# Softmax maxima handed to TensorE as two 16-bit parts, with the picks next to each other and the two turns moved

## The chip, the cores and the metric

The kernel runs on one core of a Trainium2 chip. The metric is the device time of the whole program in microseconds (us), the median of several runs. All times below are microseconds unless they are marked ns. Engines are named as the profile names them: PE (TensorE matmuls), PEld (its weight loads), DVE (VectorE), ACT (ScalarE), POOL (GpSimd), SP (SyncE).

## What is computed

A cross-attention over 32 batches, and then a feed-forward block over the tokens that a router picks. Only the attention is touched by the change. Per batch there are 112 queries and 375 context rows, 257 of an image and 118 of a text, with two separate softmaxes whose results are added:

```python
q = rms_norm(linear(x, q_w, q_b), norm_q_w).reshape(B, L, NH, HD)
k = rms_norm(linear(ctx_txt, k_w, k_b), norm_k_w).reshape(B, -1, NH, HD)
v = linear(ctx_txt, v_w, v_b).reshape(B, -1, NH, HD)
k_img = rms_norm(linear(ctx_img, k_img_w, k_img_b), norm_k_img_w).reshape(B, -1, NH, HD)
v_img = linear(ctx_img, v_img_w, v_img_b).reshape(B, -1, NH, HD)
img_x = attention(q, k_img, v_img)
txt_x = attention(q, k, v)
out = (txt_x + img_x).reshape(B, L, DIM)
return linear(out, o_w, o_b)
```

There are 16 heads of 32 numbers each, the model width is 512, everything is float32. The kernel needs the softmax's maximum of every query, head and kind of context, and subtracts it before the exponential.

## The kernel before

The 16 heads are worked on in NG = 4 groups `g` of GH = 4 heads. Phase 1 is a loop over 32 batches. Each engine has its own program, whose order is written out by hand (`body` for batches 0 to 30, of which 2 to 29 are a hardware loop, and `last` for batch 31). The programs meet only through counting semaphores: `wait_ge(semaphore, number)`. In `body(i, n, m, p, q)`, `i` is the batch in work, `n` the next one (its context is projected to keys in the same stretch), `p` and `q` the two before it (their outputs are finished there).

What a batch needs, and which engine does it:

- `scores(i, g)` (PE, L1625): queries times keys of four heads into PSUM banks 2 to 5, queries on the partitions. It serves for the maxima only.
- `group_max(i, g)` (DVE, L1151 and L1152): two reductions that read these banks, text and image maxima, into the tile `top[e]`, e = g // 2. Each head has 32 columns in `top`, of which two for each group are used. The next `scores` waits for it, since it uses the same banks.
- `turn_top(i, e)` (PE, L1636, and a copy on ACT, L834): transposes `top[e]` into `topT[e]`, so that the maxima of a head lie on its own 32 partitions. On PE there is one such turn in front of `scores(i, 3)` and one in front of `scores_T(i, 0)`.
- `scores_T(i, g)` (PE): the scores again, now with keys on the partitions. Into each PSUM bank go first the maxima with a minus sign: `topT` as the moving operand against a constant matrix that holds -1 in the rows of the wanted maximum, `pick_c` (L1660, 119 columns, text and the last image row) and `pick_img` (L1664, 128 columns). The products of keys and queries (L1654) are added on top. The matrices are held for all of the four groups and loaded anew for each matmul.
- `exps(i, g)` (ACT, L843 and L845), `sum_image` (POOL, L581, adds the two image parts of the probabilities), `add_tail` (DVE, L1157, adds the last image row), `weighted_values` (PE, L1691, in which the part with `prob_img` gives the image's sum), `normalise` (DVE, L1163, L1165, L1169), `o_hi` (ACT, L863) and `o_rest` (DVE, L1173) that make the high and the low part of the attention's result.
- `keys`, `values` and `output` (PE, L1535 to L1537): projections in three matmuls, high by high, low by high and high by low, which need `ctx_hi` (ACT, L780) and `ctx_lo` (POOL, `split_ctx`, L547, in two parts: `ctx_lo(0)` with 472 elements a partition and `ctx_lo(1)` with 1024). `keys(n, 1)` to `keys(n, 3)` need the second part. `add_bias` (DVE, L1131), `squares` (ACT, L813), `inverse_rms` (POOL, L574) and `scale_k` (DVE, L1137) finish the keys.
- `score(q)` and `ranks(q)` (DVE, L1200, L1191, L1193), `turn_score` (PE, L1641) and, in batch 30 alone, a count (PE, L1733) belong to the router. `output` and `residual` on POOL (L585, L589) are additions of 112 x 512.

PE's order in a batch is scores 0, weighted values 2 and 3 of the batch before, scores 1, values, scores 2, values, turn 0, scores 3, keys 0, turn 1, `scores_T` 0, keys 1, the score's turn, `scores_T` 1, keys 2, `scores_T` 2, weighted values 0 and 1, `scores_T` 3, output, turns, values. The waits that matter here are

```python
def scores_T(i, g):
    if g == 0:
        pe.wait_ge(s_done, 4 * i + 4)
    else:
        pe.wait_ge(exp_done, 8 * i + 2 * g)
    if g % 2 == 0:
        pe.wait_ge(topT_ready, 2 * i + 1 + g // 2)
```

## Time and profile before

| | before |
|---|---|
| median of 3 runs | 1529.23 (1525.77 to 1529.79) |
| the profiled execution | 1524.64 |
| its span, first to last instruction | 1522.9 |
| mean granted clock of PE | 0.999 |
| PE busy | 1497.2, 98% |
| PEld busy | 1186.7, 78% |
| DVE busy | 1182.6, 78% |
| ACT busy | 715.8, 47% |
| POOL busy | 688.5, 45% |

The span is that of one profiled execution, which took 1.7 more around it. The busy share is the time in which an instruction of that engine ran, also where the instruction itself was held up. The clock is the share of PE's full speed that it was granted.

### The profile page before, as it was taken

The page shows a single profiled execution, that of the slowest core. Times are in us where ns is not written, and L with a number is a line of the kernel's source. Part 1 is how long each engine was busy: PE and PEld are TensorE (multiplying, and loading weights), DVE is VectorE, ACT ScalarE, POOL GpSimd, SP SyncE. Part 2 cuts the span into 40 slices and gives each one's busy share as a digit, 9 for nine tenths or more (in the row PEclk, how much of TensorE's full clock was granted, in tenths as well). Part 3 has the DMA queues.
Part 4 walks back from the last instruction along what each step waited for, and adds up shares of the span by engine and source line. Part 5 has one row for each costly group of instructions (what it writes and reads, how often), then busy time and mean ns, then how long its engine had stood idle before and what let it go on. Part 6 is the DMA issues. An engine that isn't in the chain of part 4 may idle for free.

```text
span 1522.9 us, 41381 instructions
## 1 busy us (share of the span) xinstructions
PE 1497.2 (98%) x16220; PEld 1186.7 (78%) x16220; DVE 1182.6 (78%) x1884; ACT 715.8 (47%) x1458; POOL 688.5 (45%) x727
## 2 busy tenths in 40 slices
PE   8999999999999999999999999999999999999997
PEld 6777777777777777777777777777777787778997
DVE  6765788888888888888888888888887686554986
ACT  5874444444444444444444444444445124655431
POOL 3543344454444454444444444544445692114752
PEclk9999999999999999999999999999999999999999
DMA  8961121211111221112221112121125524010000
GB/s 262 346 207 60 39 63 52 77 56 50 56 54 59 67 66 50 56 50 62 62 70 50 56 50 62 58 75 50 56 87 154 196 111 167 28 56 29 1 1 25
DMA packets 70199, 121.04 MB, mean 79 GB/s; under 512 B 21840, under 2 KB 36528, under 8 KB 68608
## 3 DMA queue, kind: packets, MB, share of 16 engines
q1 hardware_dynamic: 69312, 117.54, 23.9%
q0 software_dynamic: 832, 2.75, 0.7%
q8 instruction: 36, 0.59, 0.2%
q14 instruction: 19, 0.16, 0.0%
HBM read 89.93 MB, written 30.34 MB: 79 GB/s over the span
## 4 chain that ended last, share of the span: by engine, by line
PE 89%; DVE 5%; ACT 3%; issue 1%; DMA 1%; POOL 1%; ACTq 0%; DVEq 0%; POOLq 0%
PE ps L1535 21%; PE ps L1536 19%; PE ps L1537 18%; PE ps L1691 10%; PE ps L1654 6%; PE ps L1625 3%; PE ps L1596 3%; PE ps L1660 2%; PE ps L1900 2%; PE ps L1917 2%; PE ps L1909 1%; PE ps L1664 1%; DMA q_dram<-q_turned 1%; DVE rec L1163 1%; PE ps L1636 0%
## 5 line engine op out<-in xcount | busy, mean ns | idle before, releaser
L547 POOL TENSOR_TENSOR ctx_lo<-ctx_raw,ctx_hi 128x472 fp32r<-128x472 f32 (+1 forms) x62 | 112.8, 1819 | 192.8 <-ACT ctx_hi L780 192.8
L1163 DVE RECIPROCAL rec<-ps 128x224 f32<-128x224 f32 x128 | 198.3, 1549 | 1.1 <-PE ps L1691 0.9
L581 POOL TENSOR_TENSOR prob_img<-prob 128x448 f32<-128x448 f32 x93 | 107.9, 1160 | 149.3 <-ACT prob L845 149.3
L1152 DVE TENSOR_REDUCE top<-ps 112x4 f32<-112x1028 f32 x128 | 156.2, 1220 | 0.0
L1151 DVE TENSOR_REDUCE top<-ps 112x4 f32<-112x472 f32 x128 | 83.1, 649 | 72.9 <-PE ps L1625 72.9
L1654 PE MATMUL ps<-q_all,k_all 32*128 32x112 f32 (+1 forms) x3072 | 125.2, 274 | 0.0
L1535 PE MATMUL ps<-w_v_img_hi,ctx_hi 128*128 128x512 f32 x256 | 107.4, 419 | 0.0
L1535 PE MATMUL ps<-w_k_img_hi,ctx_hi 128*128 128x512 f32 x256 | 107.1, 418 | 0.0
L843 ACT ACTIVATE prob<-ps 119x448 f32<-119x448 f32 x96 | 52.4, 546 | 114.8 <-PE ps L1654 114.8
L1654 PEld LDWEIGHTS ps<-q_all,k_all 32*128 32x128 f32 (+1 forms) x3072 | 105.4, 184 | 0.0
L1536 PE MATMUL ps<-w_k_img_lo,ctx_hi 128*128 128x512 f32 x256 | 101.1, 395 | 0.0
L1536 PE MATMUL ps<-w_v_img_lo,ctx_hi 128*128 128x512 f32 x256 | 101.0, 395 | 0.0
L1537 PE MATMUL ps<-w_k_img_hi,ctx_lo 128*128 128x512 f32 x256 | 100.8, 394 | 0.0
L1537 PE MATMUL ps<-w_v_img_hi,ctx_lo 128*128 128x512 f32 x256 | 100.7, 393 | 0.0
L845 ACT ACTIVATE prob<-ps 128x896 f32<-128x896 f32 x96 | 87.7, 913 | 0.0
L780 ACT ACTIVATE ctx_hi<-ctx_raw 128x472 fp32r<-128x472 f32 x64 | 52.9, 827 | 69.8 <-PE ps L1537 69.8
L1137 DVE SCALAR_TENSOR_TENSOR proj<-proj,rstd,w_img 128x512 f32<-128x512 f32 x64 | 48.0, 750 | 45.4 <-POOL rstd L574 45.4
L1537 PE MATMUL ps<-hT_hi,ring_lo 128*128 128x448 f32 x224 | 81.9, 366 | 0.0
L813 ACT ACTIVATE sq_junk<-proj 128x513 bf16<-128x513 f32 (+1 forms) x96 | 61.1, 636 | 34.8 <-DVE proj L1131 34.8
L574 POOL TENSOR_TENSOR rstd<-sq_sum,neg_half 128x1 f32<-128x1 f32 x96 | 64.8, 675 | 16.0 <-ACT sq_junk L813 16.0
L1173 DVE SCALAR_TENSOR_TENSOR oT_lo<-o_space,oT_hi 128x448 fp32r<-128x448 f32 x31 | 39.7, 1282 | 40.7 <-ACT oT_hi L863 40.7
L1157 DVE SCALAR_TENSOR_TENSOR prob_img<-prob,ones_last,prob_img 23x448 f32<-23x448 f32 x93 | 64.5, 693 | 6.1 <-POOL prob_img L581 3.1
(358 smaller groups left out, 4410.7 us busy)
## 6 DMA issues: line engine op xcount, KB each, us to landing
ctx_raw<-in_ctx_dram SPq DMA_DIRECT2D x32, 748.0 KB, 4.2
xh_dram<-xh SPq DMA_DIRECT2D x32, 448.0 KB
xc<-in_xT_dram SPq DMA_DIRECT2D x28, 256.0 KB, 4.5
q_dram<-q_turned SPq DMA_DIRECT2D x28, 256.0 KB, 4.6
q_all<-q_dram SPq DMA_DIRECT2D x32, 224.0 KB, 3.1
out_dram<-out_sb SPq DMA_DIRECT2D x32, 224.0 KB, 2.3
xh<-in_x_dram SPq DMA_DIRECT2D x31, 224.0 KB, 2.9
proj<-in_x_dram SPq DMA_DIRECT2D x21, 256.0 KB, 5.1
```

The source lines that it names most:

```text
L547: nc.gpsimd.tensor_tensor(ctx_lo[:, :, cols], ctx_raw[:, :, cols], ctx_hi[:, :, cols].bitcast(F32), ALU.subtract).then_inc(ctx_lo_done, 1)
L574: nc.gpsimd.tensor_tensor(rstd1[:, k:k + 1], sq_sum[:, k:k + 1], neg_half[:], ALU.pow).then_inc(rms_inv, 1)
L581: nc.gpsimd.tensor_tensor(prob_img[:, g % 2], image[:, 0, :], image[:, 1, :], ALU.add).then_inc(img_summed, 1)
L845: nc.scalar.activation(image.rearrange("p c (j q) -> p j c q", j=GH), ps[:, 2:6, L:3 * L].rearrange("p j (c q) -> p j c q", c=2), ACT.Exp) ...
L1151: nc.vector.tensor_reduce(rows[:, :, 2 * g], ps[0:L, 2:6, 0:TXT], AX.X, ALU.max)
L1152: nc.vector.tensor_reduce(rows[:, :, 2 * g + 1], ps[0:L, 2:6, TAIL:CTX], AX.X, ALU.max).then_inc(s_done, 1)
L1163: nc.vector.reciprocal(rec[:], bank[:, 2:4]).then_inc(norm_step, 1)
L1535: nc.tensor.matmul(o_, a_hi, b_hi, start=start, stop=False)
L1536: nc.tensor.matmul(o_, a_hi, b_lo, start=False, stop=False)
L1537: return nc.tensor.matmul(o_, a_lo, b_hi, start=False, stop=stop)
L1654: made = nc.tensor.matmul(ps[0:rows, 2 + j, c * L:(c + 1) * L], k_all[head, g, at:at + rows], q_all[head, g, :], start=False, stop=stop)
L1691: last = nc.tensor.matmul(ps[HD * j:HD * (j + 1), bank, slot * L:(slot + 1) * L], left[0:rows, cols], right[0:rows, L * j:L * (j + 1)], st ...
```

## The change

The maxima go to PE in two 16-bit parts. After every second group DVE rounds the 16 new maxima of each query to bfloat16 (`top_hi`) and writes maximum minus rounded maximum into 16 columns of `top` that were unused; `topT`, `pick_c` and `pick_img` become bfloat16, and each column of a pick matrix has two rows of -1, so that high and low part are added again in the PSUM bank. The `pick_img` matmuls stand directly behind the `pick_c` ones. On PE the first turn stays in front of `scores(i, 3)` and waits for the split; the second moves behind `keys(n, 1)`, in front of the score's turn; ACT's copy of it moves behind `squares(n, 1)`. In `last` some steps of POOL, PE, ACT and DVE change places. Two unused tiles (`pick_gap`, `top_gap`) keep the addresses of all other tiles as they were.

```diff
...
         ctx_hi = p1("ctx_hi", [P, KC, CTXC], F32R)
         ctx_lo = p1("ctx_lo", [P, KC, CTXC], F32R)
         proj = p1("proj", [P, 3, D + 1])
-        pick_c = p1("pick_c", [P, NG, CHUNK_C], F32R)
-        pick_img = p1("pick_img", [P, NG, P], F32R)
+        pick_c = p1("pick_c", [P, NG, CHUNK_C], BF16)
+        pick_img = p1("pick_img", [P, NG, P], BF16)
+        p1("pick_gap", [P, NG * (CHUNK_C + P) // 2])
         under_qT = ExitStack()
         cos_tab, sin_tab = (under_qT.enter_context(nc.sbuf_tensor(n, [L, P], F32)) for n in ("cos_tab", "sin_tab"))
         normed_last = under_qT.enter_context(nc.sbuf_tensor("normed_last", [L, D], F32))
...
         ones_last = p1("ones_last", [CHUNK_C, HD])
         ones_all = p1("ones_all", [P, HD])
         top = [p1(f"top{e}", [L, P]) for e in range(2)]
-        topT = [p1(f"topT{e}", [P, L], F32R) for e in range(2)]
+        topT = [p1(f"topT{e}", [P, L], BF16) for e in range(2)]
+        top_hi = p1("top_hi", [L, GH * 4], BF16)
+        p1("top_gap", [P, L - 8])
         prob_img = p1("prob_img", [P, 2, GH * L])
         nq_row = prob_img[:].rearrange("p a n -> p (a n)")[:, 0:D]
         prob = p1("prob", [P, 2, 3, GH * L])
...
                 for c in range(EARLY):
                     gather(c)
                 output(q)
+                residual(p)
                 pool.wait_ge(oT_lo_done, i)
+                pool.wait_ge(top_split, 2 * i + 2)
                 value_weights_lo(0, 0)
+                normalise_h(p)
                 value_weights_lo(0, 1).then_inc(w_lo_done, 1)
-                residual(p)
-                normalise_h(p)
                 token_roots(slice(0, EARLY), 1)
                 output(p)
                 pool.wait_ge(xres_loaded, 16 * i + 16)
...
                 split_ctx(n, 1)
                 value_image(i, 1)
                 turn_top(i, 0)
-                turn_top(i, 1)
                 exps(i, 0)
                 if p is not None:
                     o_hi(p)
                 squares(n, 1)
+                turn_top(i, 1)
                 exps(i, 1)
                 squares(n, 2)
                 exps(i, 2)
...
                 token_squares(0)
                 value_image(i, 1)
                 token_squares(1)
+                exps(i, 0)
                 turn_top(i, 1)
-                exps(i, 0)
                 token_squares(2)
                 exps(i, 1)
                 exps(i, 2)
...
                 rows = top[g // 2][:].rearrange("l (j r) -> l j r", j=GH)
                 nc.vector.tensor_reduce(rows[:, :, 2 * g], ps[0:L, 2:6, 0:TXT], AX.X, ALU.max)
                 nc.vector.tensor_reduce(rows[:, :, 2 * g + 1], ps[0:L, 2:6, TAIL:CTX], AX.X, ALU.max).then_inc(s_done, 1)
+
+            def split_top(i, e):
+                rows = top[e][:].rearrange("l (j r) -> l j r", j=GH)
+                high, low = rows[:, :, 4 * e:4 * e + 4], rows[:, :, 2 * NG + 4 * e:2 * NG + 4 * e + 4]
+                dve.wait_ge(s_done, 4 * i + 2 * e + 2)
+                nc.vector.tensor_copy(top_hi[:].rearrange("l (j r) -> l j r", j=GH), high).then_inc(top_rounded, 1)
+                dve.wait_ge(top_rounded, 2 * i + e + 1)
+                nc.vector.scalar_tensor_tensor(low, high, 1.0, top_hi[:].rearrange("l (j r) -> l j r", j=GH), ALU.mult, ALU.subtract).then_inc(top_split, 1)
 
             def add_tail(i, g):
                 dve.wait_ge(img_summed, 4 * i + g + 1)
...
                 else:
                     dve.wait_ge(pro_full, 2)
                     nc.vector.tensor_copy(v_tail, ps[0:B, 6, :]).then_inc(pro_done, 1)
+                split_top(i, 0)
                 group_max(i, 2)
                 if q is not None:
                     score(q)
                 group_max(i, 3)
+                split_top(i, 1)
                 if p is not None:
                     normalise(p, 3)
                 add_bias(n, 1)
...
                 group_max(i, 0)
                 o_rest(p)
                 group_max(i, 1)
+                split_top(i, 0)
                 score(q)
                 group_max(i, 2)
                 group_max(i, 3)
+                split_top(i, 1)
                 add_residual(p)
                 ln2(p)
                 ranks(q)
...
                 last.then_inc(s_full, 1)
 
             def turn_top(i, e):
-                pe.wait_ge(s_done, 4 * i + 2 * e + 2)
+                pe.wait_ge(top_split, 2 * i + e + 1)
                 if e:
                     pe.wait_ge(topT_ready, 2 * i + 1)
                 if not isinstance(i, int) or i:
...
                 for j in range(GH):
                     head = slice(HD * j, HD * (j + 1))
                     nc.tensor.matmul(ps[0:CHUNK_C, 2 + j, 0:L], pick_c[head, g, :], topT[g // 2][head, :], start=True, stop=False)
-                products(0, True)
                 for j in range(GH):
                     head = slice(HD * j, HD * (j + 1))
                     nc.tensor.matmul(ps[:, 2 + j, L:3 * L].rearrange("p (c q) -> p c q", c=2), pick_img[head, g, :],
-                                     topT[g // 2][head, :].unsqueeze(1).to_broadcast([HD, 2, L]), start=True, stop=False)
+                                     topT[g // 2][head, :].unsqueeze(1).to_broadcast([HD, 2, L]), start=False, stop=False)
+                products(0, False)
                 products(1, False)
                 products(2, True).then_inc(st_full, 1)
 
...
                 turn_top(i, 0)
                 scores(i, 3)
                 keys(n, 0)
-                turn_top(i, 1)
                 scores_T(i, 0)
                 keys(n, 1)
+                turn_top(i, 1)
                 if q is not None:
                     pe.wait_ge(pv_done, 4 * i)
                     turn_score(q)
...
                 values(i, 2, range(3, 4))
                 values(i, 1, range(0, 2))
                 scores(i, 2)
-                turn_top(i, 0)
                 values(i, 1, range(2, 3))
                 output(p, range(0, 2))
+                turn_top(i, 0)
                 scores(i, 3)
                 values(i, 1, range(3, 4))
                 output(p, range(2, 4))
-                turn_top(i, 1)
                 scores_T(i, 0)
                 pe.wait_ge(pv_done, 4 * i)
                 turn_score(q)
                 pe.wait_ge(b0_done, value_slot(i, 1)[3] + 1)
                 fill(0, 10)
+                turn_top(i, 1)
                 scores_T(i, 1)
+                pe.wait_ge(topT_ready, 2 * i + 2)
                 weighted_values(i, 0, None)
                 scores_T(i, 2)
                 pe.wait_ge(rank_done, q + 1)
...
     for w in ("wq", "wk", "wv", "wo", "w_gate", "w_up", "w_down"):
         arrays[w] = c(a[f_ + w])
     token = np.arange(L)
-    arrays["pick_rows"] = -(np.arange(P)[:, None] % HD == np.arange(2 * NG)[None, :]).astype(f)
+    parts = (np.arange(2 * NG)[None, :], 2 * NG + np.arange(2 * NG)[None, :])
+    arrays["pick_rows"] = -sum((np.arange(P)[:, None] % HD == part).astype(f) for part in parts)
     arrays["slot_far"] = np.broadcast_to(np.arange(TOPK, dtype=f) - f(FAR), (L, TOPK)).copy()
     arrays["token_no"] = token.astype(f)[:, None].copy()
     arrays["token_base"] = (L * (BPC * np.arange(NC)[None, :] + token[:, None] // TOPK)).astype(f)
```

On DVE, in the loop's body, before: from the end of `normalise(p, 2)` to the third instruction of `normalise(p, 3)`.

```order
L1169 SCALAR_TENSOR_TENSOR o_space<-o_two,v_bias 128x112
L1147 REGISTER_ALU
L1151 TENSOR_REDUCE top<-ps 112x4
L1152 TENSOR_REDUCE top<-ps 112x4
L1199 ISA
L1200 SCALAR_TENSOR_TENSOR out_sb,score_now<-xh,wr 112x512
L1147 REGISTER_ALU
L1151 TENSOR_REDUCE top<-ps 112x4
L1152 TENSOR_REDUCE top<-ps 112x4
L1161 REGISTER_ALU
L1163 RECIPROCAL rec<-ps 128x224
```

The same stretch of the changed kernel, whose line numbers are higher by 5 to 13; L1163 is the rounding here, L1165 the low part, and L1156 and L1157 are the reductions.

```order
L1182 SCALAR_TENSOR_TENSOR o_space<-o_two,v_bias 128x112
L1163 CAST top_hi<-top 112x16
L1164 REGISTER_ALU
L1165 SCALAR_TENSOR_TENSOR top<-top,top_hi 112x4x4
L1152 REGISTER_ALU
L1156 TENSOR_REDUCE top<-ps 112x4
L1157 TENSOR_REDUCE top<-ps 112x4
L1212 ISA
L1213 SCALAR_TENSOR_TENSOR out_sb,score_now<-xh,wr 112x512
L1152 REGISTER_ALU
L1156 TENSOR_REDUCE top<-ps 112x4
L1157 TENSOR_REDUCE top<-ps 112x4
```

One split now stands between `normalise(p, 2)` and the reductions of group 2; the other comes right behind the last of these rows, in front of `normalise(p, 3)`.

On PE, before: the end of `keys(n, 0)`, the second turn and `scores_T(i, 0)`.

```order
L1537 MATMUL ps<-w_k_hi,ctx_lo 118x512
L1636 MATMUL ps<-ident,top 128x112
L1660 MATMUL ps<-topT,pick_c 119x112 x4
L1654 MATMUL ps<-q_all,k_all 119x112 x4
L1664 MATMUL ps<-topT,pick_img 128x224 x4
L1654 MATMUL ps<-q_all,k_all 128x112 x8
```

The changed kernel, from the same place:

```order
L1554 MATMUL ps<-w_k_hi,ctx_lo 118x512
L1677 MATMUL ps<-topT,pick_c 119x112 x4
L1680 MATMUL ps<-topT,pick_img 128x224 x4
L1671 MATMUL ps<-q_all,k_all 119x112 x4
L1671 MATMUL ps<-q_all,k_all 128x112 x8
L1552 MATMUL ps<-w_k_img_hi,ctx_hi 128x512
```

The turn is gone from here, and the two picks (L1677, L1680) are neighbours. Behind `keys(n, 1)`, in batch 30, the changed kernel has

```order
L1554 MATMUL ps<-w_k_img_hi,ctx_lo 128x512
L1653 MATMUL ps<-ident,top 128x112
L1658 MATMUL ps<-ident,score_now 112x112
L1750 MATMUL ps<-chosen,later 112x24
L1677 MATMUL ps<-topT,pick_c 119x112 x4
```

where L1653 is the second turn and was not there before; the score's turn (L1658) and the count (L1750) stood alone.

## Rows read from the trace of the kernel before

**Rows 1.** The page's part on the chain that ended last.

```profile
PE 89%; DVE 5%; ACT 3%; issue 1%; DMA 1%; POOL 1%; ACTq 0%; DVEq 0%; POOLq 0%
```

**Rows 2.** Busy time by stretches, one whole batch; columns as in its head line.

```profile
core 0: us, PE busy (x) PEld busy (x) DVE busy (x) ACT busy (x) POOL busy (x), PEclk, DMA share, GB/s
...
714.30:747.08 32.78, 32.78 (x436) 25.66 (x435) 27.05 (x41) 15.03 (x29) 14.97 (x16) 1.00 0.19 58
```

**Rows 3.** Timeline of PE, one batch: start us, duration us, instruction.

```profile
723.68 0.26 PE L1636 MATMUL ps<-ident,top 112*128 112x112 f32 x1
...
723.87 0.43 PE L1625 MATMUL ps<-k_hi,q_hi 32*112 32x376 f32 x4
...
727.12 0.26 PE L1636 MATMUL ps<-ident,top 112*128 112x112 f32 x1
...
727.31 0.32 PE L1660 MATMUL ps<-topT,pick_c 32*119 32x112 f32 x4
...
728.36 0.50 PE L1535 MATMUL ps<-w_k_img_hi,ctx_hi 128*128 128x512 f32 x1
...
738.68 0.38 PE L1691 MATMUL ps<-prob_img,ones_all 128*32 128x112 f32 x8
```

**Rows 4.** Timeline of DVE, the same batch.

```profile
721.56 0.64 DVE L1151 TENSOR_REDUCE top<-ps 112x4 f32<-112x472 f32 x1
...
722.12 1.22 DVE L1152 TENSOR_REDUCE top<-ps 112x4 f32<-112x1028 f32 x1
...
728.07 0.34 DVE L1169 SCALAR_TENSOR_TENSOR o_space<-o_two,v_bias 128x112 f32<-128x112 f32 x1
...
730.36 1.31 DVE L1173 SCALAR_TENSOR_TENSOR oT_lo<-o_space,oT_hi 128x448 fp32r<-128x448 f32 x1 [1.35 <-ACT oT_hi L863]
...
736.12 0.75 DVE L1137 SCALAR_TENSOR_TENSOR proj<-proj,rstd,w_img 128x512 f32<-128x512 f32 x1 [1.43 <-POOL rstd L574]
...
736.90 0.68 DVE L1157 SCALAR_TENSOR_TENSOR prob_img<-prob,ones_last,prob_img 23x448 f32<-23x448 f32 x1
```

**Rows 5.** Timelines of DVE and PE in the last batch, where PE waits.

```profile
1146.01 1.22 DVE L1152 TENSOR_REDUCE top<-ps 112x4 f32<-112x1028 f32 x1
...
1147.28 0.43 PE L1625 MATMUL ps<-k_hi,q_hi 32*112 32x376 f32 x4 [0.35 <-DVE top L1152]
```

**Rows 6.** Timeline of POOL, the batch of rows 3.

```profile
721.71 1.22 POOL L547 TENSOR_TENSOR ctx_lo<-ctx_raw,ctx_hi 128x472 fp32r<-128x472 f32 x1 [5.73 <-ACT ctx_hi L780]
...
725.27 2.42 POOL L547 TENSOR_TENSOR ctx_lo<-ctx_raw,ctx_hi 128x1024 fp32r<-128x1024 f32 x1
...
730.03 1.16 POOL L581 TENSOR_TENSOR prob_img<-prob 128x448 f32<-128x448 f32 x1 [2.34 <-ACT prob L845]
...
738.20 1.15 POOL L581 TENSOR_TENSOR prob_img<-third_img 128x448 f32<-128x448 f32 x1 [2.11 <-ACT third_img L845]
```

**Rows 7.** Weight loads: groups by form, one line's range, and a timeline.

```profile
L1664 PEld LDWEIGHTS ps<-topT,pick_img 32*128 32x128 f32 x512 | 25.2, 187 | 0.0
...
L1660 PEld LDWEIGHTS ps<-topT,pick_c 32*119 32x119 f32 x512 | 23.5, 173 | 34.4 <-issue 33.8 <-ACT prob L845 0.6
...
L1901 PEld LDWEIGHTS ps<-causal,ident_bf x64: 128/130/132, 1249.4 to 1380.4; 112*112 112x112 bf16 x64
...
702.70 0.18 PEld L1660 LDWEIGHTS ps<-topT,pick_c 32*119 32x119 f32 x4 [0.36 <-issue]
...
703.00 0.20 PEld L1664 LDWEIGHTS ps<-topT,pick_img 32*128 32x128 f32 x4
```

**Rows 8.** Timeline of PE in batch 30.

```profile
1124.71 0.17 PE L1733 MATMUL ps<-chosen,later 112*112 112x24 bf16 x1
...
1124.82 0.32 PE L1660 MATMUL ps<-topT,pick_c 32*119 32x112 f32 x4
```

**Rows 9.** The instructions of line 1143.

```profile
L1143 DVE CAST k_hi<-k_tail x32: 171/172/174, 122.3 to 1138.2; 128x4 fp32r x28, 128x4 fp32r<-128x4 f32 x4
```

**Rows 10.** One line's range, then timelines of DVE and POOL.

```profile
L1173 DVE SCALAR_TENSOR_TENSOR oT_lo<-o_space,oT_hi x31: 615/1310/1311, 173.2 to 1147.1; 128x448 fp32r<-128x448 f32 x31
...
1147.14 0.61 DVE L1173 SCALAR_TENSOR_TENSOR oT_lo<-o_space,oT_hi 128x448 fp32r<-128x448 f32 x1
...
1181.98 1.00 DVE L1272 TENSOR_SCALAR chosen<-rank 112x8 bf16<-112x8 f32 x1
...
1181.67 1.28 POOL L710 TENSOR_TENSOR ring_lo<-ring,ring_lo 128x512 fp32r<-128x512 f32 x1
```

## The prediction on record

> **What bounds the kernel now.** I read the chain of waits first: TensorE (PE) holds 89% of the chain that ended last [rows 1]. Then two neighbouring batches in the table by stretches: a batch takes 32.78 us and PE is busy for 32.78 of them at a granted clock of 1.00, while VectorE (DVE) has 27.05 and GpSimd (POOL) 14.97 [rows 2]. So in the loop (batches 2 to 29) nothing is gained except by PE doing less, and anything that makes PE wait is paid in full, 28 to 30 times over. Third, the timelines, to see how late each maximum comes. The reader is to see in [rows 3, 4] that the second reduction for group 2 ends at 722.12 + 1.22 = 723.34 and that `scores(i, 3)`, which waits for it (its PSUM banks), starts at 723.87: 0.53 later. From end to start such a hand-over needs 0.05 where PE really waited (1146.01 + 1.22 = 1147.23, PE starts at 1147.28) [rows 5]. **The slack in front of the last score group is 0.48 us.** In the same way `keys(n, 1)` at 728.36 needs POOL's `ctx_lo`, which ends at 725.27 + 2.42 = 727.69 [rows 3, 6]: slack 0.67, less the hand-over.
>
> **Weight loads (gain).** Per `scores_T` the four loads of pick_c and the four of pick_img become 16-bit; there are 32 x 4 = 128 calls. Loads now: 173 ns (119 columns) and 187 ns (128 columns), while a 16-bit load of 112 columns took 130 [rows 7]. Passes follow each other every 0.10 us there (three from 702.70 to 703.00), though 112 columns stream in far less, so the loads set the pace [rows 7]. Scaled to 112 columns the 32-bit load is about 174, so 16 bits save some 44 ns at 112 columns, 0.39 ns a column; 119 + 128 columns give 0.097 us, **0.10 us a `scores_T`**, 0.41 a batch with rounding, 12.8 in all. Bounds: 0, if what counts is only the number of columns, and 0.15 (18.7 in all), if these loads vanish behind the streams. I take 0.10, from the nearest row. The Trainium skill ("TensorE: Matmul & The Clock Gate", section on LDWEIGHTS, loading the stationary operand) gives a load's time by its columns alone, columns / 1.2 in ns; by that rule this term is 0. The trace has 187 and 130 ns for a difference of 16 columns, which speaks against it. The reordering of the picks adds and removes no matmul: 0.
>
> **The moved turn.** The second turn costs 727.31 − 727.12 = 0.19 where it stands, of which a change of shape that `scores_T` has anyway is, as an estimate, 0.09: 0.10. Beside the score's turn it costs again about 0.10, as the count matmul between the same two neighbours does (1124.71 to 1124.82) [rows 3, 8]. Net 0, bounds −0.05 and +0.05. Once, in batch 30, that count matmul waits for `topT_ready`, which now comes after the second turn: +0.4.
>
> **The split on DVE.** Four instructions a batch. Alone each is as short as a cast of 128x4, 0.17 us [rows 9], and follows its neighbour with 0.04 or so for the semaphore: together 0.29 to 0.38. That would fit into the slack of 0.48. The question is whether they run alone. [Rows 10] are the evidence that they don't. L1173, a DVE instruction with two SBUF inputs, took 1.31 in the loop, with POOL's L581 running beside it (730.03 + 1.16 = 731.19 [rows 6]), and 0.61 in the last batch: it ended 0.48 after POOL's end. A DVE conversion of 112x8 to 16 bits, which should take about 0.17, took 1.00 and ended when POOL's L710 (1181.67 + 1.28) did. So one engine's instruction stands still until the other's is over. DVE's reductions, fed from PSUM, kept 0.65 and 1.22 next to L547. The new cast and subtraction are of the kind that stands still, and `split_top(i, 0)` comes at 721.56, exactly where POOL's L547 starts, at 721.71 [rows 4, 6]. 
>
> Step by step, on the clock of the batch at 714.30:
> - Cast 721.56 to 721.73. The subtraction can ask at 721.77; POOL has begun at 721.71 and holds until 722.93. It ends at 722.96. Group 2's reductions begin at 722.88 instead of 721.56, +1.32. Less the slack: **`scores(i, 3)` +0.84**.
> - The score and POOL's output addition follow, so `ctx_lo(1)` starts at 726.59 and not 725.27, and ends at 729.00. `keys(n, 1)` is due at 728.36 + 0.84 − 0.10 (load) − 0.11 (turn moved) = 728.99 and starts at 729.09: **+0.10**.
> - `split_top(i, 1)` finds that same `ctx_lo(1)` running and is held until 729.0. `normalise(p, 3)` starts at 729.15, and its third instruction (728.07 before [rows 4]) ends at 731.95 instead of 728.41, held for a while by L581. DVE is now 3.5 late; most of its idle time of 1.35 ahead of L1173 and the 0.70 that L1173 no longer loses take 1.9 of that back. But `scale_k(n, 1)` now meets POOL's residual addition and loses 0.5, so everything behind runs +2.15: `scale_k(n, 2)` 736.12 → 738.27, `add_tail(i, 1)` 736.90 → 739.05.
> - POOL's L581 for group 2 follows PE, not DVE: 738.20 → 739.01. It gets in first by 0.04 us and holds `add_tail(i, 1)`, which ends at 740.16 − 0.13 + 0.68 = 740.71. PE's image part of group 1 is due at 738.68 + 0.84 + 0.10 − 0.30 (three `scores_T`) = 739.32 and waits until 740.78: **+1.46**.
> - DVE enters the next batch late, `scores(i + 1, 1)` waits a little: **+0.08** (0 to 0.1).
>
> Per batch: 0.84 + 0.10 + 1.46 + 0.08 − 0.41 = **+2.07**. Batches 2 to 30 are 29: 60.0. Batch 0 has no `ctx_lo` in the way (−0.4), batch 1 part of it (+0.5), batch 31 has no next context (−0.3), and +0.4 of the count: +0.2. Profiled run: 1524.64 + 60.2 = 1584.8. The profiled run lies 4.6 below the median of the three runs, 1529.23, so the forecast for the median is **1589**. ACT's work and SP's queues are not changed; ACT's second topT copy moves behind squares(n, 1), into idle time, and costs nothing unless exps(i, 1) came 0.26 later (PE takes it 3 us later).
>
> **Rivals.**
> - A: as above, but `add_tail(i, 1)` wins the last race (it lost by 0.04). It then ends at 739.73 and PE waits 0.44 and not 1.46: about +1.05 a batch, 1529.2 + 30 = **1560**. For it: the tiny margin; against: each of the ends is given to 0.01 and batches repeat to that.
> - B: the subtraction wins against L547 (it lost by 0.06; if a 16-bit cast is shorter or POOL needs longer to start). Then only split 1 is held, DVE is late by less, and `add_tail(i, 1)` still meets L581: about +1.2, **1564**.
> - C, the other side: no hold at all for operations this small, since 16 elements a partition may be through before POOL takes its first. Split 0 costs 0.29 to 0.38, under the 0.48 of slack; `ctx_lo(1)` comes 0.38 later, under 0.67; only the loads remain: 1529.2 − 12.4 = **1517**. It turns on the single question of whether split 0 ends before 723.34 + 0.48 − 1.78 = 722.04. Against it: the 1.00 for 112x8.
> - D: loads of 16 bits are no faster (the rule by columns), with the holds as forecast: 1589 + 12.8 = **1602**.
> - E: one race won and the loads as forecast, or C without faster loads: gains and losses cancel, **1529**.
>
> **How the numbers follow.** Forecast 0.48 (own range 1581 to 1597), A 0.17, B 0.12, D 0.07, C 0.11, E 0.05. Two runs of this kernel can be told apart from about 0.3%, 4.6 us. Faster: C, 0.11. Same: E, 0.05. Slower: the rest, 0.84. The range leaves out C and E: from under A to just above D, 1553 to 1605.
>
> **What the profile after would show.** The split's subtraction at about 1.2 us in the loop and below 0.2 in batch 0; a mean of the cast far over 0.2, since every second one meets `ctx_lo(1)`. PE idle 0.8 to 0.9 before the last score group with DVE's reduction as releaser, and about 1.4 before the image part of group 1. Pick loads at 130 to 140 ns and `scores_T` in 0.95 us. A period of 34.85. Rival C shows itself by casts and subtractions at 0.17 and a period near 32.35; A by an idle time of 0.4 in place of 1.4; D by unchanged loads. The prediction is wrong above all if small operations slip past POOL.

## The result

The changed kernel takes 1647.93 us (median of 4; 1645.76 to 1650.04), the kernel before 1527.89 beside it: ratio 1.0785, 95% interval 1.0769 to 1.08. It is slower, as forecast, but by 120.0 us where the prediction had 60: the time lies outside the range of 1553 to 1605.

| | before | after |
|---|---|---|
| median | 1527.89 | 1647.93 |
| span of the profiled execution | 1522.9 | 1647.3 |
| mean granted clock of PE | 0.999 | 0.974 |
| PE's share of the chain [rows 1] | 89% | 55% |

The page of the changed kernel, first the busy times, then the shares of the chain that ended last:

```profile
PE 1530.3 (93%) x16220; PEld 1196.6 (73%) x16220; DVE 1351.0 (82%) x2012; ACT 713.8 (43%) x1458; POOL 689.8 (42%) x727
...
PE 55%; DVE 17%; issue 15%; POOL 6%; ACT 4%; DMA 2%; DVEq 0%; POOLq 0%; ACTq 0%
```

DVE is busy 168 us more, for 128 small instructions that were meant to take 0.17 each, 22 in all. That is the first hint that instructions stand still inside. PE's waits say where the time is lost:

```profile
PE ps L1708 <- DVE prob_img L1170: 60.6, 29, 2.2
PE ps L1642 <- DVE top L1157: 23.4, 31, 0.8
```

These are the two waits of the forecast, before the image part of group 1 (L1708) and before a score group (L1642), as total, number and longest. The second is near what was foretold (0.77 a batch for 0.8 to 0.9), the first is 2.15 in the median of the loop and not 1.46. One batch, DVE, then POOL, then PE (start us, duration us). It begins at 746.74, so 32.44 is to be taken off to compare with the clock of [rows 3, 4, 6] and of the forecast:

```profile
754.02 0.17 DVE L1163 CAST top_hi<-top 112x16 bf16<-112x16 f32 x1
754.22 1.22 DVE L1165 SCALAR_TENSOR_TENSOR top<-top,top_hi 112x16 f32<-112x16 f32 x1
755.36 0.64 DVE L1156 TENSOR_REDUCE top<-ps 112x4 f32<-112x472 f32 x1
...
759.49 2.02 DVE L1163 CAST top_hi<-top 112x16 bf16<-112x16 f32 x1
761.54 0.17 DVE L1165 SCALAR_TENSOR_TENSOR top<-top,top_hi 112x16 f32<-112x16 f32 x1
...
767.18 2.56 DVE L1142 SCALAR_TENSOR_TENSOR proj<-proj,rstd,w_txt 118x512 f32<-118x512 f32 x1
...
772.54 1.55 DVE L1170 SCALAR_TENSOR_TENSOR prob_img<-prob,ones_last,prob_img 23x448 f32<-23x448 f32 x1
```

```profile
754.18 1.22 POOL L551 TENSOR_TENSOR ctx_lo<-ctx_raw,ctx_hi 128x472 fp32r<-128x472 f32 x1 [4.63 <-ACT ctx_hi L785]
...
759.07 2.40 POOL L551 TENSOR_TENSOR ctx_lo<-ctx_raw,ctx_hi 128x1024 fp32r<-128x1024 f32 x1
...
766.79 1.29 POOL L593 TENSOR_TENSOR xh<-xh,out_bias 112x512 f32<-112x512 f32 x1
768.04 1.14 POOL L585 TENSOR_TENSOR prob_img<-prob 128x448 f32<-128x448 f32 x1
...
772.49 1.12 POOL L585 TENSOR_TENSOR prob_img<-third_img 128x448 f32<-128x448 f32 x1 [0.77 <-ACT third_img L850]
```

```profile
757.19 0.43 PE L1642 MATMUL ps<-k_hi,q_hi 32*112 32x376 f32 x4 [0.77 <-DVE top L1157]
...
760.71 0.82 PE L1671 MATMUL ps<-q_all,k_all 32*119 32x112 f32 x24
...
771.60 0.38 PE L1708 MATMUL ps<-prob,ones_txt 119*32 119x112 f32 x8
774.15 0.40 PE L1708 MATMUL ps<-prob_img,ones_all 128*32 128x112 f32 x8 [2.18 <-DVE prob_img L1170]
...
774.74 1.47 PE L1671 MATMUL ps<-q_all,k_all 32*119 32x112 f32 x24
...
776.14 0.77 PE L1552 MATMUL ps<-w_o_hi,oT_hi 128*112 128x512 f32 x1
```

Each long DVE row ends with a POOL row: the subtraction at 755.44 (POOL 755.40), the cast at 761.51 (761.47), the tail addition at 774.09, 0.48 after POOL's 773.61, like L1173 in [rows 10]. `scale_k(n, 1)` (767.18) ends at 769.74, 0.56 after the end not of the first but of the second POOL instruction beside it. The last PE rows show something else: the 24 product matmuls of a group take 0.82 at 760.71 and 1.47 here, and the first 512-column matmul of a projection 0.77 and not 0.50 [rows 3]. The granted clock in this batch, and in the microseconds after the wait (after the duration of the stretch come the busy times of PE, PEld, DVE, ACT and POOL, then the clock, here 0.95, 0.80, 0.50, 0.50, 1.00, then the DMA share and GB/s):

```profile
746.74:784.04 37.30, 34.28 (x437) 26.40 (x436) 33.64 (x47) 15.03 (x29) 15.70 (x18) 0.95 0.17 51
774.00:775.00 1.00, 0.85 (x24) 0.68 (x28) 0.97 (x3) 0.07 (x1) 0.00 (x0) 0.80 0.00 0
775.00:776.00 1.00, 1.00 (x24) 0.94 (x20) 1.00 (x1) 0.66 (x2) 0.27 (x1) 0.50 0.00 0
...
777.00:778.00 1.00, 1.00 (x4) 0.63 (x4) 1.00 (x3) 0.63 (x1) 0.21 (x1) 0.50 0.20 17
778.00:779.00 1.00, 1.00 (x6) 0.77 (x5) 1.00 (x1) 0.00 (x0) 0.94 (x1) 1.00 0.83 207
```

PE stood still from 771.97 to 774.15, and after it was granted its lower level of 1.2 GHz for some 3.4 us. Measured from one scores 0 to the next, the 28 batches of the loop take either some 35.67 us (6 batches, without such a stretch) or some 37.23 (22 batches, with one). The fall does not follow every wait of this length: the stretch from 205.06 to 240.76 has a wait of 2.14 and a clock of 1.00. The kernel before has such a standstill too, once, outside of the loop, and at a clock of 1.00:

```profile
157.13 0.43 PE L1625 MATMUL ps<-k_hi,q_hi 32*112 32x376 f32 x4 [2.13 <-ACT k_all L822]
```

All kernels of this document stand still at this place, for 2.1 to 2.4 us; the clock falls there in seven of the traces (the changed kernel's among them) and not in the other six. What decides it stays open.

### The profile page after: what moved, and what is told of

Its sections match the earlier page's. It is cut to its first block, busy times and chain, and to the rows that moved or that the text cites. A ratio compares the mean times of both kernels' runs of the same rounds, so it can differ in the third digit from the quotient of the medians.

```text
span 1647.3 us, 41594 instructions
## 1 busy us (share of the span) xinstructions
PE 1530.3 (93%) x16220; PEld 1196.6 (73%) x16220; DVE 1351.0 (82%) x2012; ACT 713.8 (43%) x1458; POOL 689.8 (42%) x727
## 4 chain that ended last, share of the span: by engine, by line
PE 55%; DVE 17%; issue 15%; POOL 6%; ACT 4%; DMA 2%; DVEq 0%; POOLq 0%; ACTq 0%
PE ps L1552 12%; PE ps L1553 11%; PE ps L1554 11%; PE ps L1708 6%; DVE top L1157 4%; POOL prob_img L585 4%; DVE rec L1176 4%; PE ps L1671 3%; DVE prob_img L1170 3%; PE ps L1613 2%; PE ps L1642 2%; PE ps L1918 2%; PE ps L1935 2%; ACT prob L850 2%; DVE top L1156 1%
## 5 line engine op out<-in xcount | busy, mean ns | idle before, releaser
L1157 DVE TENSOR_REDUCE top<-ps 112x4 f32<-112x1028 f32 x128 | 156.0, 1219 | 0.0
L585 POOL TENSOR_TENSOR prob_img<-prob 128x448 f32<-128x448 f32 x93 | 116.3, 1250 | 90.3 <-ACT prob L850 90.3
L1156 DVE TENSOR_REDUCE top<-ps 112x4 f32<-112x472 f32 x128 | 82.9, 648 | 63.7 <-PE ps L1642 63.5
L1671 PE MATMUL ps<-q_all,k_all 32*128 32x112 f32 (+1 forms) x3072 | 111.2, 278 | 0.0
L1708 PE MATMUL ps<-prob_img,ones_all 128*32 128x112 f32 x992 | 47.7, 263 | 60.6 <-DVE prob_img L1170 60.6
L1671 PEld LDWEIGHTS ps<-q_all,k_all 32*128 32x128 f32 (+1 forms) x3072 | 99.5, 192 | 0.0
L1170 DVE SCALAR_TENSOR_TENSOR prob_img<-prob,ones_last,prob_img 23x448 f32<-23x448 f32 x93 | 88.8, 955 | 5.6 <-POOL prob_img L585 2.6
```

What stands on the lines that cost most here:

```text
L585: nc.gpsimd.tensor_tensor(prob_img[:, g % 2], image[:, 0, :], image[:, 1, :], ALU.add).then_inc(img_summed, 1)
L1156: nc.vector.tensor_reduce(rows[:, :, 2 * g], ps[0:L, 2:6, 0:TXT], AX.X, ALU.max)
L1157: nc.vector.tensor_reduce(rows[:, :, 2 * g + 1], ps[0:L, 2:6, TAIL:CTX], AX.X, ALU.max).then_inc(s_done, 1)
L1170: nc.vector.scalar_tensor_tensor(prob_img[last_rows, g % 2], prob_of(g)[0][last_rows], ones_last[last_rows, 0:1], prob_img[last_rows, g % ...
L1671: made = nc.tensor.matmul(ps[0:rows, 2 + j, c * L:(c + 1) * L], k_all[head, g, at:at + rows], q_all[head, g, :], start=False, stop=stop)
L1708: last = nc.tensor.matmul(ps[HD * j:HD * (j + 1), bank, slot * L:(slot + 1) * L], left[0:rows, cols], right[0:rows, L * j:L * (j + 1)], st ...
```

## Experiments

Eleven kernels. The first four were to separate cause and place.

**split_alone**: the splits added to the kernel before, nothing else.

```diff
                 nc.vector.tensor_copy(v_tail, ps[0:B, 6, :]).then_inc(pro_done, 1)
+                split_top(i, 0)
                 group_max(i, 2)
...
                 group_max(i, 3)
+                split_top(i, 1)
```

> The kernel before with the two splits put into VectorE's order where the change has them, writing to tiles that nothing reads; TensorE, ScalarE and GpSimd are those of before. Theory (the splits are held by GpSimd's ctx_lo, VectorE comes late for the rest of the batch, and TensorE's clock falls after the long wait): the loss is all here and the loads' gain is missing, 1650 to 1670 us, with waits of about 0.8 us before the last score group and about 2 us before the image part of group 1. Rival (the loss is TensorE's: 16-bit picks among 32-bit matmuls, or the moved turn): 1528 us. Rival (VectorE merely has 0.3 to 0.4 us more to do twice a batch): 1528 to 1545 us.

Measured: 1664.85 us, ratio 1.0914 (1.0896 to 1.0932), period 37.57, waits of 0.77 and 2.03, clock 0.970. The clock falls in 27 of the 28 batches of the loop, after waits shorter than the 2.12 to 2.19 of the changed kernel: the length of the wait alone does not decide. The whole loss and more comes from two short DVE pairs whose output nobody reads. TensorE's part of the change is not to blame.

**no_split**: the opposite; the low part is left out, so the maxima that are subtracted are rounded ones. In `body`, and in the same way in `last`:

```diff
-                split_top(i, 0)
                 group_max(i, 2)
...
-                split_top(i, 1)
...
-                pe.wait_ge(top_split, 2 * i + e + 1)
+                pe.wait_ge(s_done, 4 * i + 2 * e + 2)
```

> The changed kernel without the splits: the maxima go to TensorE rounded to 16 bits, the low part is left out (it stays zero), all else is as changed. Theory: the gain of the loads alone, 0.41 us a batch, 1515 us (1509 to 1519). Rival (the loss is TensorE's own): about 1640. Rival (16-bit loads bring nothing): 1528.

Measured: 1514.04 us, ratio 0.9919 (0.9902 to 0.9935), period 32.33 for 32.78. The gain term holds: 12 to 13 us. The changed kernel's loads are 125 and 131 ns, for 173 and 187 in [rows 7] (duration min/median/max after the colon):

```profile
L1677 PEld LDWEIGHTS ps<-topT,pick_c x512: 124/125/171, 140.8 to 1284.9; 32*119 32x119 bf16 x171
...
L1680 PEld LDWEIGHTS ps<-topT,pick_img x512: 130/131/187, 140.8 to 1284.9; 32*128 32x128 bf16 x171
```

**psum_split**: same places in the order, other forms of instruction (the waits between them and the form of the last batch are left out here).

```diff
-                nc.vector.tensor_copy(top_hi[...], high).then_inc(top_rounded, 1)
-                nc.vector.scalar_tensor_tensor(low, high, 1.0, top_hi[...], ALU.mult, ALU.subtract).then_inc(top_split, 1)
+                nc.vector.tensor_reduce(rounded, high.unsqueeze(3), AX.X, ALU.max).then_inc(top_rounded, 1)
...
+                in_bank = ps[0:L, 7, 448:464].rearrange("l (j r) -> l j r", j=GH)
+                nc.vector.tensor_reduce(in_bank, rounded.unsqueeze(3), AX.X, ALU.max).then_inc(top_rounded, 1)
...
+                nc.vector.scalar_tensor_tensor(low, high, 1.0, in_bank, ALU.mult, ALU.subtract).then_inc(top_split, 1)
```

> The changed kernel, the splits at the same places but in a form that has never two operands in SBUF and no cast: a reduction over one element rounds, a second one puts the rounded part into PSUM, and the subtraction reads it there; three instructions for two, 0.17 each. (The last batch keeps the SBUF operand.) Theory (held at the port that VectorE shares with GpSimd): no instruction of the split takes over 0.25 us; 0.55 to 0.6 us stand in a slack of 0.48, so 1515 to 1530 us. Rival (VectorE's added work by itself, or its place in the order): 1640 or more.

Measured: 1521.24 us, ratio 0.997 (0.996 to 0.9981), period 32.57. Its DVE groups (busy, then mean ns of one):

```profile
L1168 DVE TENSOR_REDUCE ps<-top_hi 112x16 f32<-112x16 bf16 x62 | 11.1, 178 | 2.1
L1164 DVE TENSOR_REDUCE top_hi<-top 112x16 bf16<-112x16 f32 x64 | 10.6, 166 | 1.1
L1173 DVE SCALAR_TENSOR_TENSOR top<-top,ps 112x16 f32<-112x16 f32 x62 | 10.6, 171 | 2.1
L1173 DVE SCALAR_TENSOR_TENSOR top<-top,top_hi 112x16 f32<-112x16 f32 x2 | 1.4, 702 | 0.1
```

Three instructions in the same place as the two, at 0.17 each, next to the same GpSimd work, cost 0.24 us a batch. The two that kept both operands in SBUF (last batch) have a mean of 0.70: one took 0.17, the other 1.23. So neither the amount of work nor its place loses the 120 us by itself; it takes the place together with an instruction that is a cast or has both operands in SBUF.

**filled**: work for PE inside the long wait.

```diff
+                        if slot == 2 and n is not None and g == 1:
+                            for _ in range(18):
+                                nc.tensor.transpose(ps[:, 7, 448:512], ident[0:64, :], ident[0:64, 0:64])
                         if slot == 2 and n is not None:
                             pe.wait_ge(tail_added, 4 * i + g + 1)
```

> The changed kernel with 18 matmuls that nothing reads in front of the wait for the image part of group 1, some 2 us of work in a wait of 2.15. Theory (the granted clock falls because TensorE idles that long, and the slow stretch costs 1.57 us in 22 batches): the clock stays at 1.00, every period is 35.7 us, and the time is about 1613 us. Rival (the slow stretch has another cause): 1648 us or more, the clock below 1 as before.

Measured: 1613.92 us, ratio 1.0579 (1.0561 to 1.0597), 34.0 us less than the changed kernel, with more work. All periods of the loop are 35.65 to 35.73, and the clock of the same 200 us is 1.00; first this kernel, then the changed one:

```profile
700.00:900.00 200.00, 189.50 (x2561) 147.43 (x2560) 183.21 (x251) 82.66 (x164) 87.06 (x84) 1.00 0.18 54
```

```profile
700.00:900.00 200.00, 183.71 (x2360) 141.45 (x2361) 176.38 (x245) 81.01 (x157) 79.83 (x82) 0.96 0.16 49
```

The 18 matmuls took 1.35 us of the wait, and PE still stood for 0.89 in the median before the image part. So the slow stretch is the clock's, it comes from PE standing still that long, and it costs 22 x 1.56 = 34 us. (Outside of the loop the clock fell once here too, after 2.19 at the place named above.)

**moved0, moved1, moved_both**: the splits at times when GpSimd is idle, one by one and together. moved_both is both edits:

```diff
-                split_top(i, 0)
                 group_max(i, 2)
+                split_top(i, 0)
...
-                split_top(i, 1)
                 if p is not None:
                     normalise(p, 3)
+                split_top(i, 1)
...
-                turn_top(i, 0)
                 scores(i, 3)
+                turn_top(i, 0)
                 keys(n, 0)
```

> The changed kernel with the first split behind group 2's reductions and, on TensorE, the first turn behind scores 3. Theory: the first split now runs where GpSimd is idle (between ctx_lo(0) and the output addition), no wait before the last score group; the second split is still held by ctx_lo(1), 1.6 us or so, and VectorE comes late for the image part of group 1, by less than before (VectorE is about 0.8 less late): a wait there of 0 to 1 us, clock 1.00, 1520 to 1550 us. Rival (the first split's hold alone makes the loss): 1515.

> The changed kernel with the second split behind the normalisation of group 3, where GpSimd is idle. Theory: the first split is held as before, so 0.77 us before the last score group and ctx_lo(1) late; the rest of VectorE's batch is late by less than before, the wait for the image part of group 1 is between 0 and 1.5 us and too short for the clock to fall: 1530 to 1580 us. Rival (the second split's hold alone makes the loss): 1515 to 1520.

> Both moves together. Theory: no split is held (0.17 each), TensorE waits nowhere in the loop, the loads' gain is left: 1514 us as without splits, at most 1518, faster than the kernel before by 0.7 to 0.8%. Rival (0.3 us of work on VectorE at any place reaches TensorE): over 1520.

Measured: moved0 1599.64 us (1.047, 1.0452 to 1.0489); moved1 1544.2 (1.0105, 1.0088 to 1.0122); moved_both 1514.08 (0.9918, 0.99 to 0.9935). Their longest-lasting waits in the loop, moved0 and then moved1:

```profile
PE ps L1708 <- DVE prob_img L1170: 62.9, 29, 2.3
```

```profile
PE ps L1642 <- DVE top L1157: 23.4, 31, 0.8
```

Each split has its own wait. Against the 32.33 of no_split, the periods are 33.31 with the first split held (+0.98), 34.80 with the second held and no slow stretch (+2.47), 35.67 with both (+3.34): nearly a sum. My number for moved0 was 50 us or more too low. I had thought that a DVE less late by 0.8 would come to the image part less late too. It doesn't: the rounding of the second split takes 1.96 to 2.00 there, `scale_k(n, 1)` takes 2.56 again, and of the 28 waits of 2.24 in the loop 10 are followed by a fall of the clock. In moved_both PE waits for no split in the loop, every period is 32.3, and the split costs nothing:

```profile
L1163 DVE CAST top_hi<-top x64: 161/167/1405, 133.9 to 1142.3; 112x16 bf16<-112x16 f32 x64
```

```profile
L1165 DVE SCALAR_TENSOR_TENSOR top<-top,top_hi x64: 174/176/177, 134.3 to 1142.5; 112x16 f32<-112x16 f32 x64
```

The median is 167 ns. The one of 1405 is the second rounding of batch 0, outside of the loop, where POOL's `ctx_lo(1)` comes at another time: it ends at 138.74, POOL's 136.28 + 2.43 at 138.71. So the new places are free by the loop's timing, and not for good. This is the fastest version with the full two-part maxima, 0.8% faster than before; psum_split, at the old places, is 0.3% faster than before.

**port_given**: GpSimd lets `scale_k(n, 1)` go first.

```diff
                     residual(p)
+                    pool.wait_ge(scaled, 3 * n + 1)
                 sum_image(i, 1)
```

> The changed kernel with one wait more on GpSimd: ahead of the image sum of group 1 it waits for scale_k(n, 1), so that this VectorE instruction gets its turn between GpSimd's residual addition and the image sum. Theory (scale_k(n, 1) took 2.56 us because two GpSimd instructions in a row went ahead of it, the step by which the forecast of 1.46 us became 2.15): it takes about 1.5, everything behind it on VectorE comes 1.1 us earlier, add_tail(i, 1) is ahead of GpSimd's third image sum by a microsecond and takes 0.68 and not 1.55, the wait in front of the image part falls from 2.15 to 0.2 to 0.5 us, the clock stays at 1.00, the period is near 33.9 us and the time 1555 to 1570 us. Rival (VectorE would have got its turn anyway, and the time is spent elsewhere): 1640 us or more.

Measured: 1580.87 us, ratio 1.0351 (1.0336 to 1.0366), period 34.59, clock 0.998. The median of `scale_k(n, 1)` is now 1.46, its range:

```profile
L1143 DVE SCALAR_TENSOR_TENSOR proj<-proj,rstd,w_txt x32: 750/1455/1664, 115.9 to 1181.6; 118x512 f32<-118x512 f32 x32
```

and the wait before the image part fell from 2.15 to 1.07, so by the 1.10 that the second POOL instruction had taken. But not to 0.2 to 0.5, and the time is above the 1555 to 1570 that was expected: `add_tail(i, 1)` is still held. DVE and then POOL, same batch:

```profile
736.34 1.57 DVE L1171 SCALAR_TENSOR_TENSOR prob_img<-prob,ones_last,prob_img 23x448 f32<-23x448 f32 x1
```

```profile
736.29 1.13 POOL L585 TENSOR_TENSOR prob_img<-third_img 128x448 f32<-128x448 f32 x1 [0.77 <-ACT third_img L851]
```

0.05 between them, as in the changed kernel (772.54 and 772.49). I had taken L585 to follow PE. In the late batch it follows DVE: ScalarE squares the keys that `add_bias(n, 2)` gave it before it takes up the exponentials of group 2, and both the sum and, over POOL's reciprocal root, `scale_k(n, 2)` start from there. In the changed kernel:

```profile
770.37 0.64 ACT L818 ACTIVATE sq_junk<-proj 128x513 bf16<-128x513 f32 x1 [3.10 <-DVE proj L1136]
...
771.42 0.91 ACT L850 ACTIVATE third_img<-ps 128x896 f32<-128x896 f32 x1
```

port_given shows it: counted from the start of the batch (711.68 here, 746.74 in the changed kernel) the sum starts at 24.61 and not at 25.75, earlier by the same 1.14 as the DVE side, though PE's order is the same. The two arrive at a fixed distance when both are late, and rival A could not win.

**reduce_cast**: the rounding as a reduction, the subtraction as it is.

```diff
-                nc.vector.tensor_copy(top_hi[...], high).then_inc(top_rounded, 1)
+                nc.vector.tensor_reduce(top_hi[...], high.unsqueeze(3), AX.X, ALU.max).then_inc(top_rounded, 1)
```

> The changed kernel with the rounding as a reduction over one element in place of the cast, the subtraction with both operands in SBUF as it is. If both kinds of instruction are held (theory), the rounding now takes 0.17 and the subtraction behind it is held instead, at both places, and the time stays at 1648 us within 1%. If it was the cast alone that was held at the second split, the subtraction there takes 0.17 too and the time falls to about 1545.

Measured, one run: 1644.5 us, periods of 35.7 and 37.2 as in the changed kernel. The rounding has a mean of 0.17, and the subtraction took over what the cast had been held for (174/1212/1829 ns, where the changed kernel has a median of 177):

```profile
L1165 DVE SCALAR_TENSOR_TENSOR top<-top,top_hi x64: 174/1212/1829, 131.2 to 1274.2; 112x16 f32<-112x16 f32 x64
```

**adjacent_only and turn_moved**: the two rearrangements of the change, each alone in the kernel before. The edits are a move of the `pick_img` loop in front of `products(0, ...)`, and of `turn_top(i, 1)` behind `keys(n, 1)` (PE) and `squares(n, 1)` (ACT).

> The kernel before with nothing changed but the order of the picks: the image picks directly behind the text picks, still 32-bit. Theory (the loads' size makes the gain, not the order): 1526 us, within 0.3%. Rival (the order makes part of it, since the pass of 224 columns now hides another load): 1520 or less.

> The kernel before with nothing changed but the second turn, moved on TensorE in front of the score's turn and on ScalarE behind squares(n, 1). Theory: net 0, 1527 us within 0.3%. Rival (the new neighbours save or cost 0.1 us a batch): 3 us to either side.

Measured: 1527.12 (1.0001, 0.9993 to 1.001) and 1527.01 (1.0, 0.9991 to 1.0008), periods 32.78 and 32.77. Both are nothing, as costed.

## Why the prediction was right in direction and wrong in size

**Weight loads.** Right: 0.45 us a batch measured (32.78 to 32.33), 0.41 foretold; 125 and 131 ns. In part that is luck: the working puts a 32-bit load of 112 columns at 174 ns, but the two rows it starts from (173 at 119 columns, 187 at 128) make it 162, and then 0.07 a `scores_T` and 0.28 a batch. The 16-bit loads were shorter than the 130 to 140 expected, which made up for it. The rule by columns alone of the Trainium skill ("TensorE: Matmul & The Clock Gate", section LDWEIGHTS, loading the stationary operand) does not hold here: the same 119 columns took 173 ns in 32 bits and 125 in 16. Order and turn: right, 0 each.

**First split.** Right to 0.04 us. On the forecast's clock the subtraction ended at 723.00 (foretold 722.96), group 2's reductions began at 722.92 (722.88), `ctx_lo(1)` at 726.63 (726.59). `scores(i, 3)` starts at 724.75 (724.71), 0.88 later than before. In moved1, where this split alone is held, the whole costs 0.98 a batch (0.84 + 0.10 foretold).

**Second split.** Right: held until 729.07 (729.0), `normalise(p, 3)` at 729.20 (729.15).

**The step that failed first** is "`scale_k(n, 1)` now meets POOL's residual addition and loses 0.5". It met it, but POOL's next instruction, the image sum of group 1, was ready and went ahead of the waiting DVE as well. It lasted 2.56 and not about 1.5, and ended at 737.30. In the kernel before it ended at 733.15 + 0.94 = 734.09, so the +2.15 of the forecast had it at 736.24:

```profile
733.15 0.94 DVE L1137 SCALAR_TENSOR_TENSOR proj<-proj,rstd,w_txt 118x512 f32<-118x512 f32 x1
```

`scale_k(n, 2)` behind it started at 739.32 (738.27).

**A second step failed with it**, "POOL's L581 for group 2 follows PE, not DVE: 738.20 → 739.01". It started at 740.05. This is what makes the first error dear: had POOL's sum run from 739.01 to 740.16, `add_tail(i, 1)`, which came at 740.10, would, as an estimate by the forecast's own rule, have ended at its 740.71 all the same. As it is, it ended at 741.65. PE itself was on time. The last matmul before the image part, in the kernel before and in the changed one (771.60 above) is

```profile
738.49 0.38 PE L1691 MATMUL ps<-prob,ones_txt 119*32 119x112 f32 x8
```

so PE is there 771.60 - 32.44 - 738.49 = 0.67 later (0.64 foretold), and it starts the image part at 741.71 (740.78), 0.93 too late. (The idle time of the profile, 2.15 in the median, is counted from the end of a matmul, the 1.46 of the forecast from the start that PE's order would have given.) port_given shows both steps: 1.07 us of wait go away when POOL stands back, and POOL's sum moves with DVE. The +0.08 for the next batch came to 0.02. In the whole that is period 35.67 for 34.85, 0.82 x 28 = 23 us.

**What was missing from the sum altogether** is the clock. All rows of before have it at 1.00, since PE never stood still in the loop; I treated a wait as costing its own length. After waits of 2.12 to 2.19 it fell in 22 of 28 batches, 34 us (filled). The Trainium skill ("TensorE: Matmul & The Clock Gate", Part 1: The HAM clock gate) says that a monitor passes or halves the clock by how busy the engine has been of late; the trace agrees, with 0.50 after the wait. I had not applied that to a wait that my own forecast made. Whether the wait of 1.46 that I had foretold would have done it is not shown: in the loop of port_given, with waits of 1.02 to 1.09, it never fell, and neither did it after the standstill of 1.38 that every trace has in front of batch 0.

For the 28 batches of the loop the sum then closes: 28 x 2.07 = 58 foretold, and 23 and 34 more, make 115, and in the profiled executions the loop took 115.1 longer. Outside of it the profiled execution is another 9.2 longer, where the forecast has 2.3 (batch 30 among it, with +1.9 for +2.5, and 3.0 before batch 0, which starts at 127.5 here and, behind the same instructions, at 123.9 in filled); these ends are not explained one by one.

**The rivals.** C, that such small operations slip past POOL, fell at the first row. It was right in its arithmetic: with nothing held the time is 1514 to 1521 (1517 foretold). A and B hung on margins of 0.04 and 0.06 us. Both were lost in all 28 batches of the loop; in the batch shown by 0.05 and 0.04. In batch 30, where `scale_k(n, 1)` took 1.55, A's race was won, and PE waited 0.18. D fell with the loads. The range was too narrow on its upper side: it took the forecast and added only the loads, and no case let a second POOL instruction go ahead of DVE or gave a wait of PE a consequence for its clock.

Not tested: what lets DVE in between two POOL instructions (here a gap on POOL did), and what decides between the batches with and without a fall of the clock at equal waits.

## What to carry to other kernels

Before a short VectorE instruction is put into an order, look at what GpSimd is doing at that moment: with two operands in SBUF, or as a cast, 0.17 us of work here took up to 2.0 us, and as much as GpSimd has ready in a row can go ahead of it. The repair that paid most was a place: a few instructions further down the same splits were free and the change was worth 0.8%. Forms that are not held (psum_split) got back all of it but 0.24 us a batch. When an engine comes late, ask of each instruction that it meets whether that one is late for the same reason: the two then meet again. And a wait of TensorE that grows to two microseconds has to be priced with the slower clock that may follow it, here about 1.56 us each time.

## What was not expected of the hardware

- An instruction of VectorE that waits for the shared access is not next in line: two GpSimd instructions that followed each other directly went ahead of it. It took 2.56 us, against 0.75 at the least (batch 0) and 1.46 in port_given, where GpSimd left a gap behind the first.
- After a standstill of 2.0 to 2.25 us TensorE was granted 0.50 of its clock for about 3.4 us, though not each time: in 22 of the loop's 28 batches in the changed kernel (2.12 to 2.19), in 27 of split_alone (2.02 to 2.04), in 10 of moved0 (2.23 to 2.25). With 18 small matmuls inside the same stretch it was granted 1.00 in all 28.
- Reductions over a single element, rounding to 16 bits, took 0.17 us beside GpSimd's work and were never held (psum_split, x64, mean 166 ns).
